# The last fold over heads of a routed attention layer: from VectorE to TensorE, with a few steps moved

## The reference

```python
def _L0_ffn_ref(x, Wq, Wk, Ws, Wd, Wv, Wo):      # H, DH, E = 8 heads, 64, 5 experts
    q = (x @ Wq).reshape(b, t, h, dh).transpose(0, 2, 1, 3)
    k = (x @ Wk).reshape(b, t, h, dh).transpose(0, 2, 1, 3)
    wv = _topk_mask(gl_v, SEL) * jax.nn.sigmoid(gl_v)
    xv = jnp.einsum('btd,edk->btek', x, Wv)
    v = jnp.einsum('bthe,btek->bhtk', wv, xv)
    probs = jax.nn.softmax(jnp.einsum('bhid,bhjd->bhij', q * scale, k), axis=-1)
    attn = jnp.einsum('bhij,bhjd->bihd', probs, v)
    mask_o = _topk_mask((x @ Wd).reshape(b, t, h, e), SEL)
    out = jnp.einsum('bthe,bthk,ekd->btd', mask_o, attn, Wo)
    return out
```

## Time and profile before

| | us |
|---|---|
| median of 3 runs | 1505.91 (1503.93 to 1517.23) |
| the profiled execution: its time | 1514.99 |
| its span, first to last instruction | 1513.3 |
| PE busy | 1252.8 (83%) |
| PE weight loads busy | 967.0 (64%) |
| DVE busy | 1039.2 (69%) |
| ScalarE busy | 863.1 (57%) |
| GpSimd busy | 834.7 (55%) |
| mean granted TensorE clock | 0.902 |

### The profile page before, as it was taken

The page is one execution under the profiler, slowest core; times in us unless marked ns, Lnnn a source line. Parts: engine busy times, 40 slices in busy tenths (PEclk is TensorE's granted clock), DMA queues, the critical chain, the costliest instruction groups (busy, mean ns, idle before and its releaser), DMA issues. The chain is left out here.

```text
span 1513.3 us, 37262 instructions
## 1 busy us (share of the span) xinstructions
PE 1252.8 (83%) x14513; PEld 967.0 (64%) x14513; DVE 1039.2 (69%) x2439; ACT 863.1 (57%) x2737; POOL 834.7 (55%) x867
## 2 busy tenths in 40 slices
PE   5888889878878888787898878788887578999897
PEld 4667667665656676566677756666665156777676
DVE  4457886877876786878668779887654857555552
ACT  3687765536458458657837645563544555545441
POOL 3038596695476438742763883884231767443432
PEclk7578988989988889999789899999998689999999
DMA  6000000000000000000000000001001000000000
GB/s 162 5 2 1 2 1 2 2 1 2 21 2 1 21 2 2 2 22 2 1 21 2 1 2 2 17 8 47 1 21 37 20 2 2 9 9 16 9 9 15
DMA packets 26694, 19.05 MB, mean 13 GB/s; under 512 B 6520, under 2 KB 24216, under 8 KB 26392
## 3 DMA queue, kind: packets, MB, share of 16 engines
q1 hardware_dynamic: 24936, 15.78, 3.6%
q10 hardware_dynamic: 1584, 0.89, 0.2%
HBM read 12.73 MB, written 3.93 MB: 11 GB/s over the span
## 5 line engine op out<-in xcount | busy, mean ns | idle before, releaser
L1206 ACT ACTIVATE arena<-bank 128x512 f32<-128x512 f32 (+5 forms) x361 | 186.1, 546 | 248.7 <-PE bank L507 68.6
L1619 DVE TENSOR_REDUCE arena<-pair 128x8 f32<-128x1024 f32 (+2 forms) x224 | 241.1, 1096 | 124.8 <-PE pair L557 47.7
L2238 POOL TENSOR_SCALAR_AFFINE_SELECT arena<-arena 128x1024 f32<-128x1024 f32 (+1 forms) x128 | 143.4, 1131 | 262.2 <-ACT arena L1423 138.1
L2293 POOL TENSOR_TENSOR arena<-arena 128x512 f32<-128x512 f32 x160 | 186.1, 1163 | 52.8 <-DVE arena L1736 46.3
L1253 ACT ACTIVATE arena<-pair,arena 77x128 f32<-77x128 f32 x512 | 178.5, 371 | 33.2 <-DVE arena L1619 24.1
L2298 POOL TENSOR_TENSOR arena<-arena 128x512 f32<-128x512 f32 x128 | 180.5, 1410 | 10.1
L502 PE MATMUL bank<-ident 128*128 128x128 f32 x780 | 125.5, 302 | 9.0 <-POOL subscale L2189 4.3
L2314 POOL TENSOR_TENSOR arena<-arena 128x512 f32<-128x512 f32 x64 | 67.3, 1065 | 110.9 <-ACT arena L1206 72.6
L502 PEld LDWEIGHTS bank<-ident 128*128 128x128 f32 x780 | 109.3, 209 | 26.6 <-issue 11.2
L1588 ACT ACTIVATE arena<-pair 77x1024 f32<-77x1024 f32 x64 | 63.1, 1016 | 83.0 <-PE pair L1128 74.9
L1206 ACT ACTIVATE arena<-bank,arena 128x128 f32<-128x128 f32 x256 | 77.5, 508 | 54.8 <-PE bank L909 35.6
(11 more groups left out here) (298 smaller groups left out, 3051.9 us busy)
## 6 DMA issues: line engine op xcount, KB each, us to landing
arena<-in_ctx_turned SPq DMA_DIRECT2D x16, 154.0 KB, 3.1
arena<-in_x SPq DMA_DIRECT2D x8, 256.0 KB, 4.2
out<-arena SPq DMA_DIRECT2D x8, 256.0 KB, 2.3
spill<-arena SPq DMA_DIRECT2D x7, 256.0 KB, 2.0
arena<-spill SPq DMA_DIRECT2D x7, 256.0 KB, 4.2
arena<-in_ctx SPq DMA_DIRECT2D x8, 154.0 KB
arena<-in_ctx_turned SPq DMA_DIRECT2D x1, 1232.0 KB, 6.0
wexp<-in_L_ffn_expert_w SPq DMA_DIRECT2D x1, 512.0 KB, 4.3
```

The source lines that it names most:

```text
L1206: return act.activation(dst, src, func, bias=bias, scale=scale)
L1619: return dve.tensor_reduce(dst, src, X, op, **kw)
L2238: return pool.affine_select(out=e, in_=e, compare_op=ALU.is_ge, fill=0.0, base=0, pattern=[[0, 8], [1, 128]], channel_multiplier=-1)
L2293: pool.tensor_tensor(into, xvs[:, b, ex * SHD:(ex + 1) * SHD].unsqueeze(1).broadcast_to([128, SH, SHD]), gates[g % 2][:, b, 0:SH, ex].unsq ...
```

## The change

PE now does the last fold. DVE folds 8 heads into 4 and 4 into 2 as before, but the second of these now writes both halves to `ys` (its two buffers become the two halves of one block), and the third fold is gone. For each 128 columns PE multiplies both halves by the identity, the second product accumulating on the first, so the bank gets the transpose of their sum. The fold into `ys` now waits until PE has read `ys` for the block just before. In part C the statistics step of DVE also waits for `ln3.ready` of the group before. In the table ORDER the strings of part A are rearranged; those of parts B and C, and the table FILL, are the same. Counted by the n-th occurrence of each letter, steps move by 1 to 3 places mostly, by up to 11 on PE, 9 on DVE, 7 on ScalarE, and on GpSimd by up to 19 for the steps that write constants at the start.

```diff
     ("A", "vector"):
-        "aiaabbwwwwwwwwbcbbcbbcbccdbaabbcbddbcdeddbdbcebechhhhahheachhbbdbhhcbhhhcbhhbbchhhhhdddbedhhdcdahhhh"
+        "aiabbawwwwwwwwcbbbcbbcbccdbaabbcbdbdcdeddbdbecbehchhhhahahechbdhbbhchbhhhcbhhbbhhhchhddbdedhhcddahhhh"
...
                     pe.wait_ge(f0_ys, C.next(f0_ys))
                     for t in range(3):
-                        ins = pe.transpose(o.bank[:, tokens(t)], ys[:, b % 2, tokens(t)], ident[:])
+                        for i in range(2):
+                            ins = mm(o.bank[:, tokens(t)], ys[:, i, tokens(t)], ident[:], start=(i == 0), stop=(i == 1))
                     ins.then_inc(o.full, 1)
...
                     tt(oprod[:, :, 0:256], oprod[:, :, 0:256], oprod[:, :, 256:512], ALU.add).then_inc(C.give(dve_step), 1)
                     dve.wait_ge(dve_step, C.last(dve_step))
                     yield
-                    tt(oprod[:, :, 0:128], oprod[:, :, 0:128], oprod[:, :, 128:256], ALU.add).then_inc(C.give(dve_step), 1)
-                    if b >= 2 or g:
-                        y = E["f0", g, "ys", b - 2] if b >= 2 else E["f0", g - 1, "ys", SEQS + b - 2]
+                    if b or g:
+                        y = E["f0", g, "ys", b - 1] if b else E["f0", g - 1, "ys", SEQS - 1]
                         dve.wait_ge(y.full, y.n)
-                    dve.wait_ge(dve_step, C.last(dve_step))
-                    tt(ys[:, b % 2, 0:NV].rearrange("p (e k) -> p e k", e=SE), oprod[:, :, 0:64], oprod[:, :, 64:128], ALU.add)\
-                        .then_inc(C.give(f0_ys), 1)
+                    tt(ys[:, :, 0:NV].rearrange("p i (e k) -> p e i k", e=SE),
+                       oprod[:, :, 0:128].rearrange("p e (i k) -> p e i k", i=2), oprod[:, :, 128:256].rearrange("p e (i k) -> p e i k", i=2),
+                       ALU.add).then_inc(C.give(f0_ys), 1)
...
                 dve.wait_ge(c_added, g + 1)
+                if g:
+                    dve.wait_ge(ln3.ready, g)
                 stats(ln3, x).then_inc(C.give(ln3.var), 1)
```

## The result

The changed kernel takes 1532.03 us (median of 20 runs, 1518.11 to 1537.18) against 1512.05 us of the kernel before (20 runs, 1501.59 to 1520.47). The ratio is 1.012, 95% interval 1.0098 to 1.0142: slower by 20 us. The forecast was 1510 us with a range to 1532, so the time lies on the upper edge of the range, and on the far side of the 1% that the likeliest case promised. The three runs of before that were known then had a median of 1505.91, 6 us under that of 20. As a change the forecast was +4 us, and the measurement is +20 us by the medians and +18 by the ratio.

The account below looks back on a forecast made before the run. No engine was full from 126 to 1040 us; PE had least room, 149 us idle. Longer burst +15, fold waits -6, freed VectorE -5, moves 0: +4 us, 1505.9 + 4 = 1510 us, range 1490 to 1532.

Parts of the forecast that it names:

- the likeliest case: Whole kernel: +4 us, 1510 us in terms of the median, range 1497 to 1521; chance 0.60.
- What the edit removes: VectorE's fold L1785 goes, 32 times, 28.8 us; the new last fold priced as L1780, 1.33 us, no change.
- What it adds: PE's burst before the output product: 3 records become 12, +1.39 us a block (1.02 to 1.81), +44 us of PE time.
- What of it is on the path: Edited chain, 126 to 1040 us: longer burst +15, PE's fold waits -6, VectorE's freed queue -5, sum +4 us.
- The moved steps: Rearranged part A order: small moves both ways that no row prices, taken as 0 with +-10 us for the range.
- PE pays in full: Rival: PE's queue decides every block, +44 - 6 - 5 = +33 us, 1539 us (1521 to 1545); chance 0.22.
- The relief decides: Rival: VectorE and its port shared with GpSimd limit, longer burst hides in idle time; -22 us, 1484 us; chance 0.13.
- The fourfold price: Rival: six products on PE cost four times a transpose, +4.0 us a block, 1572 us; chance 0.02.
- The clock: Rival: more products raise the granted clock in the changed stretch, 4 us per 0.01; -8 us, 1502 us; chance 0.03.
- The wait in layer 3: VectorE's added statistics wait in layer 3 costs nothing, its counter being given a whole group before, 35 us.

Follow-up runs that it names:

- The relief alone: Kernel before with the new two-step VectorE fold, old order, three transposes of the first half only, second half left out of the sum: 1503.73 us, ratio 0.9925.
- Six products alone: Kernel before, all three VectorE folds kept, each transpose replaced by two plain products, the second overwriting the first: 1533.29 us, ratio 1.0136.
- The fold alone: Changed kernel with all four strings of part A in the order of before: 1512.08 us, ratio 1.0004 to the kernel before.
- the kernel with the tail put back: Changed kernel with all four part A strings as before from near the end of group 6 on: 1518.28 us, ratio 1.0031 to the kernel before.
- PE's piece put back: Changed kernel with places 691 to 698 of PE's part A string as before, burst ahead of L731 and L910: 1532.95 us, ratio 1.0109 to the kernel before.

## Why the prediction came out at the edge of its range

**What the edit removes: right.** 28.8 us of VectorE's folds, of which I let 11 reach the end (6 by PE's waits, 5 by the queue). The relief alone measured 0.75%, 11 us (6 to 16). The new fold costs 1.39 us where I took L1780's 1.33.

**What it adds: right in kind, 21% too long.** Two records for each product held (384). I took L623's 0.164 us a record, 1.97 us a burst and +1.39; it is 0.144, 1.73 and +1.15, between that and the lower end of 1.60. Why the records keep a closer pace here than in L623's bursts of eight, no run shows.

**What of it is on the path: the sum of the edit held, its parts within wide errors.** Of 44 us of added PE time I let 15 reach the end, a third. Six products alone measured +21 us (14 to 27) for 36 us of PE time, more than half, so the share was probably too low and the too long burst made up for part of it. The fold alone came out at +0.04% (-0.32 to +0.40) against my +4 us, 0.3%: inside the error.

**The moved steps: the term that failed.** "I see no row that prices the moves; I take 0 and keep +-10 us for the range." They cost 1.2% with the new fold (18 us over the fold alone, 11 to 24 by the intervals) and 2.7% with the old one (41 us). Both are outside +-10. That the time still comes out at the edge of the stated range is luck: the range reached to +26 us, but for the sake of PE's longer burst, which with the relief costs nothing. The moves are small, 1 to 3 places mostly, and of both signs, and I let that stand for a small effect. It doesn't follow: all the engines run in a fixed order and wait for each other, and the effect of the whole set is not that of the steps that were looked at. At the first block the reading was right: in the changed kernel the fold ends at 125.66 us and the burst starts at 126.59 without a wait, so PE is the one that is late. But one block was no sample of 32. Over all of them PE waits 11.8 us for the fold in the changed kernel and 2.7 in the fold without moves, so in other blocks the new order sends PE there too early. Nor is that wait the price of the moves: the kernel with the tail put back waits 10.7 us and loses 0.31%, the one with PE's and ScalarE's moves alone 8.7 us and loses 2.26%.

**The rivals.** "PE pays in full" named 1539 us and came nearest in time, yet its mechanism isn't what happened: PE's burst costs 58% of its added length alone, and nothing net with the relief. Its stated range, 1521 to 1545, doesn't come out of the bounds either; they give 33 - 11 = +22 to 58 - 11 = +47 us, 1528 to 1553. "The relief decides" is half right: the relief pays back the burst, no more. The fourfold price falls with 0.144 us a record. The clock moved a little, the way that rival said: 0.909 for 0.902 in the profiled executions, 0.92 for 0.91 in the changed part, and 0.916 in the mean of the 20 runs, where the kernel before has 0.897 to 0.905 in the other three jobs. By my price of 4 us for each 0.01 that would be some 4 to 8 us of gain inside the measured loss (an estimate; no run separates it).

**The wait in layer 3: right at nothing**, within that error, by the fold without moves, which contains it.

**What stays open.** Which moves do the harm, and through which wait. Roughly two thirds of it lie in the last fifth of the order. Neither of the two places that I tried carries it alone, the pair was not tried, and strings of PE or ScalarE alone can't run. Whether PE's and ScalarE's moves are bad in themselves or only beside unmoved strings is open too. That the moved order was right for some other durations than the chip's would fit all of this and was not tested. No kernel tried beats the one before with the whole sum computed: the fold in the old order (1.0004) and with one piece moved (0.9986) are both within the measurement.

## What to carry to other kernels

Where an edit comes with a rearranged order, price the two apart before anything else: here the edit was worth 0.0% and the order +1.2%, and from the diff alone the edit looked like the change. In a hand-ordered program with several in-order engines, many small moves of both signs needn't cancel, so give them a range wider than the largest of the priced terms (15 us here, where the moves measured 18), not a small one around zero. And a late step with a low clock beside it in the timeline is a place and not yet a cause: put that step back in both orders before you believe it, and where two late steps meet at one place, put back each alone and both together.

## What the runs showed of the hardware

- An fp32 product of 128x128 by the identity leaves two records and a transpose of the same tile one. In bursts, a transpose took 0.19 us (18.5 us / 96) and a product 0.29 us (55.3 us / 192), a factor of 1.5. The Trainium skill, "TensorE: Matmul & The Clock Gate" (Terms), has the transpose mode 4x faster for FP32; the measured factor here is 1.5.
- A VectorE operation with a single SBUF input can take several times as long beside GpSimd's work (that GpSimd held it is inferred, not tested): L1706, a TENSOR_SCALAR of 128x32, took 0.18 us in one kernel and 1.09 us in the other, with GpSimd at work in both stretches. The long one ended at 980.21 us, as an operation of GpSimd (L2295, 979.11 to 980.17) that had started beside it ended. The Trainium skill, "SBUF — State Buffer" (SBUF: two separate sides), names operations in a 2-port mode beside those with two SBUF inputs as ones that contend for the pair. The 1.09 us agree with that, though no run shows whether L1706 ran in such a mode.
- In the changed kernel a wait of PE of 1.68 us, ended at 980.72, stood just ahead of a fall of the granted clock to 0.50 from 982 to 990 us, with two more waits of 0.63 and 1.35 us inside it; operations there took 1.9 times as long (1.96 for 1.01, 3.66 for 1.93 us). With PE's piece put back the clock of 980 to 992 is 0.83 for 0.57, and the time of the whole kernel is as it was, 1.0109 for 1.012.
